# Gathering three tables' rows of the last tile in two halves of 64 samples

## What is computed

```python
e = jnp.stack([tbl_0[ids[:, 0]], ..., tbl_25[ids[:, 25]]], axis=1)
interactions = jnp.einsum('bnd,bmd->bnm', combined, combined)
z = concatenate([dense, interactions[:, TRIU_I, TRIU_J]], axis=1)
h = jnp.concatenate([z, r_dense_features], axis=1)
h = jnp.maximum(h @ W_top1 + b_top1, 0.0)
h = jnp.maximum(h @ W_top2 + b_top2, 0.0)
y = h @ W_top3
```

## Time and profile before

| | us |
|---|---|
| median of 3 runs (lowest to highest) | 101.78 (101.72 to 101.84) |
| the profiled execution's own time | 102.27 |
| its span, first to last instruction | 100.5 |
| outside the span (own time less span) | 1.77 |
| granted TensorE clock, mean | 0.998 of full speed |

### The profile page before, as it was taken

The page is one execution under the profiler, slowest core; times in us unless marked ns, Lnnn a source line. Parts: engine busy times, 40 slices in busy tenths (PEclk is TensorE's granted clock), DMA queues, the critical chain, the costliest instruction groups (busy, mean ns, idle before and its releaser), DMA issues.

```text
span 100.5 us, 3478 instructions
## 1 busy us (share of the span) xinstructions
PE 94.2 (94%) x1525; PEld 77.6 (77%) x1525; DVE 52.6 (52%) x117; ACT 50.6 (50%) x84; POOL 61.3 (61%) x66
## 2 busy tenths in 40 slices
PE   5999999999999999999999989999999897998990
PEld 1347788668888888899888878898898795987970
DVE  4599959999999969975000610262022601126020
ACT  2888999897499299384211242007400543003521
POOL 1488877777778877777777777777777760000000
PEclk9999999999999999999999999999999999999999
DMA  2999999999999999512222222212122221000000
GB/s 55 243 325 257 299 281 277 258 249 278 238 264 265 268 328 373 162 52 59 52 59 52 59 52 62 59 52 59 52 59 59 52 52 26 7 7 0 7 0 1
DMA packets 5366, 13.46 MB, mean 134 GB/s; under 512 B 1732, under 2 KB 1992, under 8 KB 5223
## 3 DMA queue, kind: packets, MB, share of 16 engines
q1 hardware_dynamic: 3260, 9.11, 33.0%
q0 software_dynamic: 1920, 3.94, 14.8%
q10 hardware_dynamic: 170, 0.18, 0.8%
HBM read 13.23 MB, written 0.00 MB: 132 GB/s over the span
## 4 chain that ended last, share of the span: by engine, by line
POOL 55%; issue 19%; PE 14%; DMA 8%; POOLq 1%; ACT 0%
POOL rows_sb L312 55%; DMA rows_sb<-tbl,ids_sb 5%; PE ps_a L402 3%; PE ps_gram L376 3%; DMA ids_sb<-ids 2%; PE ps_h L439 2%; PE ps_h L468 1%; POOLq L128 1%; PE ps_rows L451 1%; PE ps_rows L354 1%; PE ps_a L415 1%; PE ps_rows L456 1%; PE ps_a L425 1%; ACT y_sb L741 0%; PE ps_gram L395 0%
## 5 line engine op out<-in xcount | busy, mean ns | idle before, releaser
L312 POOL DMA_INDIRECT rows_sb<-tbl,ids_sb x60 | 60.9, 1015 | 20.4 <-issue 17.1
L339 PE MATMUL ps_a<-onehot,part_sb 125*128 125x512 f32 (+1 forms) x208 | 45.0, 366 | 0.4 <-ACT part_sb L668 0.2
L339 PEld LDWEIGHTS ps_a<-onehot,part_sb 125*128 125x128 f32 x208 | 34.1, 188 | 8.2 <-DVE onehot L575 1.2
L575 DVE TENSOR_SCALAR onehot<-idrow,row_id 125x1024 fp32r<-125x1024 int16 (+1 forms) x41 | 26.6, 708 | 1.5 <-DMA idrow<-ids_by_table 1.5
L584 DVE TENSOR_TENSOR part_sb<-table_sb,part_sb 125x512 fp32r<-125x512 f32 x22 | 14.4, 683 | 2.7 <-ACT part_sb L668 2.6
L690 ACT COPY xt<-ps_a 128x512 f32<-128x512 f32 (+1 forms) x13 | 7.6, 584 | 13.7 <-PE ps_a L339 13.5
L697 ACT COPY xt<-ps_rows 128x512 f32<-128x512 f32 (+3 forms) x17 | 9.9, 584 | 8.6 <-PE ps_rows L354 8.6
L376 PE MATMUL ps_gram<-xt 128*27 128x27 f32 x1024 | 13.4, 195 | 0.5 <-issue 0.2
L376 PEld LDWEIGHTS ps_gram<-xt 128*27 128x27 f32 x1024 | 11.1, 108 | 3.3 <-issue 0.6
L638 DVE TENSOR_SCALAR table_sb<-ps_a,columns_sb 128x128 f32<-128x128 f32 x8 | 2.4, 346 | 20.4 <-PE ps_a L425 17.3
L668 ACT CAST part_sb<-table_sb 125x1024 fp32r<-125x1024 f32 (+1 forms) x12 | 11.7, 979 | 0.6 <-DMA table_sb<-tbl 0.6
(11 more groups left out here) (41 smaller groups left out, 43.3 us busy)
## 6 DMA issues: line engine op xcount, KB each, us to landing
table_sb<-tbl SPq DMA_DIRECT2D x11, 448.0 KB
idrow<-ids_by_table SPq DMA_DIRECT2D x5, 256.0 KB, 7.5
w_sb<-w SPq DMA_DIRECT2D x1, 1280.0 KB, 9.9
rows_sb<-tbl,ids_sb POOLq DMA_INDIRECT x60, 5.7
table_sb<-tbl SPq DMA_DIRECT2D x10, 52.0 KB
w_sb<-w SPq DMA_DIRECT2D x1, 512.0 KB, 9.6
dense_sb<-dense_by_column SPq DMA_DIRECT2D x1, 256.0 KB, 7.6
idrow<-ids_by_table ACTq DMA_DIRECT2D x1, 128.0 KB, 2.8
```

The source lines that it names most:

```text
L312: pool.indirect_dma_start(rows_sb[:, t % ROWS_RING, k, :], None, tables[f], bass.IndirectOffsetOnAxis(ids_sb[:, t, f:f + 1], 0),).then_inc ...
L339: last = pe.matmul(ps_a[:, i % 2, a:b], parts_sb[part][:, w, c * D:(c + 1) * D], unit_onehot(u, c)[:, member, a:b], start=(part == HIGH an ...
L575: dve.tensor_scalar(unit_onehot(u, c), idrow[0:VP, w, 0:n, :], row_id[0:VP, first + c:first + c + 1], None, ALU.is_equal).then_inc(onehot_ ...
```

## The change

In words:

- Tile 3 has groups of 4, 4, 4 and 3 tables again (12 to 15). Group 15 gathers only the first 64 samples of the last three tables. A new group 16 gathers the same tables' other 64 samples, into the first 64 partitions of a free place of the ring, with ids of its own (`second_ids`, 64 by 3) that SP loads after the identity. POOL issues 57 gathers of 128 rows and 6 of 64.
- SP's first DMA brings only tile 0's ids; the ids of the other tiles come in a DMA after the first table's, and POOL waits for them ahead of its first gather of tile 1.
- `turn_group` and `copy_group` take 64 samples for groups 15 and 16.
- For tile 3, quarters 0 and 1 of `gram` take samples 0 to 63, and wait for one copied group fewer; quarter 2 waits for the last one. The samples' order in `ps_gram` is changed for this tile, and `copy_last_z` puts it back.
- On PE, `turn_group(16)` comes behind `gram(3, 1)`, and `layer3([0, 1])` and `layer1_dense(3, 0)` between the two first quarters.

```diff
+GROUPS = [(t, sum(GROUP_SIZES[:i]), k) for t in range(TILES) for i, k in enumerate(GROUP_SIZES)]
+HALF_TILE = P // 2
+FIRST_HALVES = len(GROUPS) - 1
+SECOND_HALVES = len(GROUPS)
+GROUPS.append(GROUPS[FIRST_HALVES])
+HALVED = GATHERED[-GROUP_SIZES[-1]:]
+FREES_ROWS = 8
...
-            sp.dma_start(ids_sb[:, :, :], ids).then_inc(ids_landed, 16)
+            sp.dma_start(ids_sb[:, 0, :], ids[:, 0, :]).then_inc(first_ids_landed, 16)
             load_first_table(sp, 0, VP_A)
+            sp.dma_start(ids_sb[:, 1:, :], ids[:, 1:, :]).then_inc(ids_landed, 16)
...
             sp.dma_start(ident_sb[:, :], identity).then_inc(ident_landed, 16)
+            sp.dma_start(second_ids_sb[:, :], second_ids).then_inc(second_ids_landed, 16)
             for h in range(TABLE_RING, NOH):
                 load_table(h)
...
-            pool.wait_ge(ids_landed, 16)
-            for g, (t, first, n) in enumerate(GROUPS):
+            pool.wait_ge(first_ids_landed, 16)
+            for g, (t, first, n) in enumerate(GROUPS[:SECOND_HALVES]):
+                if (t, first) == (1, 0):
+                    pool.wait_ge(ids_landed, 16)
...
-                        rows_sb[:, t % ROWS_RING, k, :], None, tables[f],
-                        bass.IndirectOffsetOnAxis(ids_sb[:, t, f:f + 1], 0),
+                        rows_of(g)[:, k - first, :], None, tables[f],
+                        bass.IndirectOffsetOnAxis(ids_sb[0:HALF_TILE if g == FIRST_HALVES else P, t, f:f + 1], 0),
                     ).then_inc(group_landed[g], 16)
+            pool.wait_ge(second_ids_landed, 16)
+            pool.wait_ge(group_turned, FREES_ROWS + 1)
+            for k, f in enumerate(HALVED):
+                pool.indirect_dma_start(
+                    rows_of(SECOND_HALVES)[:, k, :], None, tables[f],
+                    bass.IndirectOffsetOnAxis(second_ids_sb[:, k:k + 1], 0),
+                ).then_inc(group_landed[SECOND_HALVES], 16)
...
                 for slot in range(n):
-                    last = pe.transpose(ps_rows[:, g % 2, slot * P:(slot + 1) * P],
-                                        rows_sb[:, t % ROWS_RING, first + slot, :], ident)
+                    last = pe.transpose(ps_rows[:, g % 2, slot * w:(slot + 1) * w],
+                                        rows_of(g)[:, slot, :], ident_sb[0:w, 0:w])
...
-                    pe.wait_ge(group_copied, GROUPS_UP_TO[t])
+                    pe.wait_ge(group_copied, GROUPS_UP_TO[t] - (t == TILES - 1))
...
+                if t == TILES - 1 and quarter == QUARTERS // 2:
+                    pe.wait_ge(group_copied, GROUPS_UP_TO[t])
                 for s in range(first, first + SPQ):
                     for j in range(P // NPAD):
-                        b = t * P + j * NPAD + half * SPB + s
+                        if t == TILES - 1:
+                            b = t * P + half * HALF_TILE + j * SPB + s
+                        else:
+                            b = t * P + j * NPAD + half * SPB + s
...
             turn_group(15)
-            turn_group(16)
             layer1_pairs(2, 3)
             gram(3, 0)
+            layer3([0, 1])
+            layer1_dense(3, 0)
             gram(3, 1)
-            layer3([0, 1])
+            turn_group(16)
             layer2(2, 0)
-            layer1_dense(3, 0)
             gram(3, 2)
             gram(3, 3)
             layer2(2, 1)
...
-                act.copy(zt[:, (TILES - 1) % 2, c, :], last_z(c)).then_inc(last_copied, 1)
+                act.copy(zt[:, (TILES - 1) % 2, c, :].rearrange("p (h j s) -> p h j s", h=2, s=SPB),
+                         last_z(c).rearrange("p (j h s) -> p h j s", h=2, s=SPB)).then_inc(last_copied, 1)
```

More of the change, by code:

```diff
@@ L74 @@
 GROUP_SIZES = [4, 4, 4, 3]
[L75 to L78, removed]
+GROUPS = [(t, sum(GROUP_SIZES[:i]), k) for t in range(TILES) for i, k in enumerate(GROUP_SIZES)]
+assert sum(GROUP_SIZES) == len(GATHERED)
+HALF_TILE = P // 2
[4 more added lines that the diff above has]
+FREES_ROWS = 8
+assert GROUPS[FREES_ROWS][:2] == (TILES - 2, 0) and GROUPS[FREES_ROWS][2] >= len(HALVED)
 FREED_BY = {g: max(e for e, (s, j, m) in enumerate(GROUPS) if s == t - ROWS_RING and j < i + k)
@@ L124, in packed_w1, with build @@
     return np.ascontiguousarray(np.stack(chunks, axis=1))
-def build(nc, dense_by_column, ids, ids_by_table, tables, w1, w2, columns, identity, out):
+def build(nc, dense_by_column, ids, second_ids, ids_by_table, tables, w1, w2, columns, identity, out):
     with ExitStack() as ctx:
@@ L142, in build @@
         ids_sb = sb("ids_sb", [P, TILES, F], I32)
+        second_ids_sb = sb("second_ids_sb", [HALF_TILE, len(HALVED)], I32)
         dense_sb = sb("dense_sb", [D, B], F32)
@@ L175, in build @@
         SPB = NPAD // 2
+        first_ids_landed = sem("first_ids_landed")
         ids_landed = sem("ids_landed")
+        second_ids_landed = sem("second_ids_landed")
         ident_landed = sem("ident_landed")
@@ L237, in h2_block, with rows_of, samples_of @@
             return ps_h2[:, 0, m * P:(m + 1) * P]
+        def rows_of(g):
+            t, first, n = GROUPS[g]
+            if g == SECOND_HALVES:
+                return rows_sb[0:HALF_TILE, (t - 1) % ROWS_RING, 0:n, :]
+            return rows_sb[0:HALF_TILE if g == FIRST_HALVES else P, t % ROWS_RING, first:first + n, :]
+        def samples_of(g):
+            t = GROUPS[g][0]
+            middle = t * P + HALF_TILE
+            return (middle if g == SECOND_HALVES else t * P), (middle if g == FIRST_HALVES else (t + 1) * P)
         def last_z(c):
@@ L352, in turn_group @@
                 pe.wait_ge(group_landed[g], 16 * n)
+                first_sample, end = samples_of(g)
+                w = end - first_sample
                 for slot in range(n):
-                    last = pe.transpose(ps_rows[:, g % 2, slot * P:(slot + 1) * P],
-                                        rows_sb[:, t % ROWS_RING, first + slot, :], ident)
+                    last = pe.transpose(ps_rows[:, g % 2, slot * w:(slot + 1) * w],
+                                        rows_of(g)[:, slot, :], ident_sb[0:w, 0:w])
                 last.then_inc(group_turned, 1)
@@ L696, in copy_group @@
                 act.wait_ge(group_turned, g + 1)
-                act.copy(xt[:, t * P // RUN:(t + 1) * P // RUN, slots, :].rearrange("p q n r -> p n q r"),
-                         ps_rows[:, g % 2, 0:n * P].rearrange("p (n q r) -> p n q r", n=n, r=RUN)).then_inc(group_copied, 1)
+                first_sample, end = samples_of(g)
+                act.copy(xt[:, first_sample // RUN:end // RUN, slots, :].rearrange("p q n r -> p n q r"),
+                         ps_rows[:, g % 2, 0:n * (end - first_sample)].rearrange("p (n q r) -> p n q r", n=n, r=RUN)) \
+                   .then_inc(group_copied, 1)
             def copy_z(t):
@@ L811 @@
     arrays["ids"] = np.ascontiguousarray(ids.reshape(TILES, P, F).transpose(1, 0, 2))
+    last_half = B - HALF_TILE
+    arrays["second_ids"] = np.ascontiguousarray(ids[last_half:, HALVED])
     arrays["w1"] = packed_w1(np.asarray(inputs["W_top1"]))
@@ L821 @@
     out = nc.dram_tensor("y", (B, 1), F32, kind="ExternalOutput").ap()
-    build(nc, a["dense_by_column"], a["ids"], a["ids_by_table"], [a[f"tbl_{f}"] for f in range(F)],
+    build(nc, a["dense_by_column"], a["ids"], a["second_ids"], a["ids_by_table"], [a[f"tbl_{f}"] for f in range(F)],
           a["w1"], a["w2"], a["columns"], a["identity"], out)
```

## The result

| | before | after |
|---|---|---|
| median (lowest to highest) of 18 runs each, us | 101.88 (101.34 to 103.25) | 102.60 (101.93 to 103.76) |
| ratio after to before, 95% interval | | 1.0073 (1.005 to 1.0097) |
| the profiled execution's own time, its span | 102.27, 100.5 | 102.27, 100.5 |

The change costs 0.7 us where I forecast a gain of 0.25. Comparisons leave out runs more than 1.5% above a kernel's fastest, so the ratio of a kernel that spreads widely rests on a part of its runs; where ratio and median part, both are given. They show where things stand in the kernel, and the medians carry the difference.

A forecast was written before the change was run, and what follows sets the result against it. PE and POOL's gathers end nearly together, with at most about 1.2 us of PE's waiting for rows to win. Products -0.09 and ids -0.16 gave -0.25 us: median 101.78 to 101.5, range 101.1 to 102.5.

The forecast's parts named there:

- The price of a half gather: POOL's busy time for a gather of 64 rows: bounds 0.54 and 0.95 us, middle 0.74 taken.
- Rival 1: Slower: a gather costs by the instruction, felt at the transposes of groups 15 and 16; +0.67 us, 102.4; chance 0.31.
- the ids' 0.16: Gain in us from a smaller first load of ids, which lets POOL's gathers start sooner.
- its terms of 0.54 and 0.29: At a half gather of 0.95 us: products ending 0.54 us later, plus PE's 0.29 us wait for group 16.
- The formula itself: Shift of the products' end, 3H - 2.31 us: -0.09 for H of 0.74, +0.54 for 0.95.
- H: Busy time of one gather of 64 rows on POOL, taken as 0.74 us.
- Part 1: First halves: PE can turn group 15 at 81.24 + 3H, which is 83.46 for H of 0.74.
- Part 2: PE from group 15's first transpose to the products' end: 6.06 us instead of 5.52, for added transposes and parted quarters.
- Part 3: Second halves on POOL: ready at 86.58, PE there at 86.92, so no wait for group 16; copies covered.
- Part 4: Split ids: first gather starts sooner, the whole stream shifts, -0.16 us; SP's two extra DMAs cost nothing.
- Part 5: New order of samples in tile 3's products and `copy_last_z`: costs nothing.
- What follows the products: Pack, layers and store after the last products: claimed unchanged, 10.9 us of the span.

The follow-up runs named there:

- e3_full_gathers: The changed kernel with three whole gathers for the last tables in place of six halves, and no load of the halves' ids; ratio to before 1.0061.
- f1_full_whole_ids: The changed kernel with three whole gathers in place of six halves and all ids in one load; ratio to before 1.0044.
- a0_after: The changed kernel unaltered, run once more with a second profile; ratio to before 1.0107.
- e7_whole_ids: The changed kernel with all ids in one load again, everything else as changed; ratio to before 1.0085.
- e1_price_by_rows: The kernel before with fifteen unread gathers of 16 to 128 rows added at POOL's end; 128 rows took 0.08 us more than 16.
- e5_other_fetch_times: The changed kernel with two warm-up products replaced by sixty tiny ones, to move PE's later instruction loads; ratio to before 1.0146.
- e4_fill_waits: The kernel before with split ids and ready PE work put into its two waits for rows; ratio 1.0054, median 103.82 against 101.97 us.

## Why the prediction was wrong

**The price of a half gather** is the step that failed: "No row is nearer to one end, so I take the middle, 0.74." It is 0.90. My argument against the upper end was a POOL instruction of 0.13 us, so that 0.8 us were "spent on what a gather does". That was true, and the inference wrong: what a gather does hardly depends on its rows. The middle between two mechanisms was a value that neither of them gives. Rival 1, with the chance of 0.31, is what came, its 102.4 lying 0.2 below the median of 102.60; without the ids' 0.16, which no run shows at the end, it had said 102.6, and so the stated range ended at 102.5. That its number came so near is partly luck, since its terms of 0.54 and 0.29 were too small and a shorter stretch behind the products made up for it (below). The formula itself stands better than its input: with whole gathers, H = 0.95, it gives +0.54 before the ids, and `e3_full_gathers` and `f1_full_whole_ids` measure 0.6 and 0.4%, some 0.62 and 0.45 us.

**Part 1** holds as a formula. 81.24 + 3H with H = 0.90 is 83.94; POOL's stream stood 0.48 earlier in this execution (78.45 against 78.93), which makes 83.46, and PE turned group 15 at 83.40. The forecast's wait of 0.3 ahead of it was 0.79.

**Part 2** was 6.06 and came to 6.21 and 6.19 in `e3_full_gathers` and `f1_full_whole_ids`, where no wait lies within it, and to 6.38 in after less its wait. A group of half transposes is 0.29 to 0.33 (`a0_after` too), not 0.24: the shorter rows bought no shorter transposes. Three steps that I took over unchanged, pairs 0.76, dense part 0.54 and layer 2's half 1.00, take 0.87, 0.64 and 1.09 in the new order (`e3_full_gathers`), together +0.30; after, `a0_after` and `f1_full_whole_ids` show the same within 0.01. Each now stands behind another step than in before, and why that costs a tenth is not shown. The parted quarters were 0.53 and 0.68 there, +0.13 over the 1.08 where I took 0.20 (after has 0.68 and 0.75), and the later pair gave 0.25 back (1.21 for 1.46).

**Part 3** said no wait for group 16, and the wait was 0.54, then 1.07. With H = 0.90 the step's own sum gives 78.93 + 5 x 1.20 + 0.90 + 1.71 = 87.54, less 0.48 is 87.06, and PE arrived at 87.72 - 0.54 = 87.18. So even the right price made no wait: the term that failed is the landing, 1.58 after the end of the gather, which an instruction load beside it stretched to 84.49 + 3.09 - 85.40 = 2.18. Rival 1's wait of 0.29 thus had the right place and the wrong cause. That the copies are covered, and that nothing waits behind the gathers on POOL, held.

**Part 4**: the first gather started at 3.37 instead of 3.51, 0.14 for my 0.16. Over all profiles it is more, a median of 3.19 us in the nine with the split against 3.56 in the eight without, but little of it is left at the end: the gathers of the last three tables start at 78.64 against 78.74, with single profiles from 77.69 to 79.21. That "the whole stream shifts" is thus not shown, and the split alone gave 1.0038 and 0.9995. Its cost "at nothing" left out the second lookup, ahead of which PE waited 0.47, 0.52 and 1.36 in three of the profiles with the split; but `e7_whole_ids` has 0.36 there without it.

**Part 5** held: ACT's last copies take 0.27 us in both kernels.

**What follows the products "is unchanged"** was wrong. It went from 10.89 to 10.18 in the profiled pair. Before stood there for 0.45 to 0.64 at an instruction load; in after that load was some 2.3 us old when PE came to the place where `a0_after` stands (about 91.7 against 89.41), and PE went on. Some of the change's loss is hidden there. With the terms as they stand in the profiled pair, 3 x 0.90 - 2.31 = +0.39, +0.32 for part 2, +0.54 for the wait, -0.48 for POOL's stream and -0.71 for the tail (what follows the products) give +0.06, and the two executions are equally long. The medians say +0.72, since what helped this execution of after is not there in all: POOL's stream is on the median no more than 0.1 earlier, and in `a0_after` the tail is 10.56. The last tile's layer 2 starts at 95.21 and 94.61 in two profiles of before, at 95.19 and 96.35 in two of after, 0.86 later on the mean.

So the gain that was there to win, 1.2 us of waiting for rows, was not reached, since the first halves come only some 3 x 0.05 us sooner; PE's added work and the second halves' wait were paid for nothing.

## What to carry to other kernels

Measure what a gather costs at several sizes before it is split: here 16 rows cost nine tenths of 128, so splitting three gathers brought the first halves some 0.15 us sooner and put the start of the last gather 3.06 us later. Filling a wait for data on the engine that sets the end won nothing in two tries here, so look for waits without a named cause behind it before counting on its length. Where a landing is longer than its neighbours, look in the DMA view for what shared the queues with it, instruction loads among them.

## What the runs showed of the hardware that was not expected

**A gather's price is nearly flat:** POOL is busy for 0.87, 0.88, 0.91, 0.92 and 0.95 us for 16, 32, 64, 96 and 128 rows of 512 bytes (`e1_price_by_rows`), with 0.30 of gap behind each.

**An instruction load lengthens a landing beside it:** 2.3 to 2.4 us became 3.1 to 3.7 in five profiles, and the long landing moved when `e5_other_fetch_times` moved the load. The Trainium skill's page DMA: Bandwidth & Descriptors (Why a DMA increments its semaphore by 16 and not by 1) says that only the full count of all sixteen engines means that the data has landed. By that page one engine kept busy by the load would be enough to delay the landing; no run here shows the single engine.

**PE can stand still beside an instruction load, in or behind a stretch of small matmuls:** it stood for 0.18 to 2.06 us and went on 2.2 to 2.8 us after a 16 KB load began. The Trainium skill's page Runtime: NRT & Kernel Launch (Instruction fetch mechanics) calls the cost of crossing a 16 KB boundary of the instructions mostly hidden. If instructions are what PE lacked, it was not hidden in these stretches, and the measurement decides. That they were is inferred from the timing in all these profiles; no run took the loads away.

**The longest of these stalls was followed by a lower clock:** in `e4_fill_waits` PE was busy for 0.16 of 2.20 us, then worked until 90 us at a granted clock of 0.91 on the mean, and the clock was 0.50 (1.2 GHz) from 90 to 92 us. One profile has this; that the stall brought the clock down is not shown by another.
